# First MoE: three tiles turned ahead of routing, lists loaded between x tiles, and the tail's order of work changed

## The reference

```python
logits = (flat @ router_w).astype(jnp.float32) + router_bias
probs = jax.nn.softmax(logits, axis=-1)
top_w, top_i = jax.lax.top_k(probs, TOPK)               # TOPK = 2 of E = 16
norm_w = top_w / (jnp.sum(top_w, axis=-1, keepdims=True) + 1e-06)
combine = jnp.sum(jax.nn.one_hot(top_i, E) * norm_w[..., None], axis=1)
routed = combine[:, E - 1:E] * flat                      # the last expert is the identity
for e in range(E - 1):
    y = jax.nn.silu(flat @ expert_gate_w[e]) * (flat @ expert_up_w[e]) @ expert_down_w[e]
    routed = routed + combine[:, e:e + 1] * y
gate = conv1d(hidden_states, conv_w)                     # causal, KS = 3 taps
shared = jax.nn.silu(gate) * (hidden_states @ shared_up_w) @ shared_down_w
return shared + routed
```

## Time and profile before

| what | us |
|---|---|
| median of 3 runs (1435.53, 1438.24, 2847.57) | 1438.24 |
| the profiled execution's own time | 1436.97 |
| its span, first to last instruction | 1435.2 |
| TensorE matmul busy in it | 1321.7 (92%) |
| VectorE (DVE) busy | 1008.5 (70%) |
| ScalarE (ACT) busy | 614.5 (43%) |
| GpSimd (POOL) busy | 573.0 (40%) |

### The profile page before, as it was taken

The page is one execution under the profiler, slowest core; times in us unless marked ns, Lnnn a source line. Parts: engine busy times, 40 slices in busy tenths (PEclk is TensorE's granted clock), DMA queues, the critical chain, the costliest instruction groups (busy, mean ns, idle before and its releaser), DMA issues.

```text
span 1435.2 us, 30723 instructions
## 1 busy us (share of the span) xinstructions
PE 1321.7 (92%) x11824; PEld 1087.4 (76%) x11824; DVE 1008.5 (70%) x2390; ACT 614.5 (43%) x1034; POOL 573.0 (40%) x460
## 2 busy tenths in 40 slices
PE   5959998856999999999999899999999999999998
PEld 2449988435888788788788688788788776699974
DVE  5756465377977877876876867877887868655745
ACT  4726555411343333333434344333333656666641
POOL 0536270631323332331441533552553436272635
PEclk9979999978999999999999999999999999999999
DMA  9977695920000000000001000000000038586845
GB/s 324 382 233 247 214 345 205 305 90 1 2 2 2 1 2 1 2 1 2 34 12 61 2 1 2 16 16 1 16 16 1 31 97 302 192 272 214 272 134 154
DMA packets 113628, 150.99 MB, mean 105 GB/s; under 512 B 12240, under 2 KB 96080, under 8 KB 113488
## 3 DMA queue, kind: packets, MB, share of 16 engines
q1 hardware_dynamic: 99088, 113.36, 24.0%
q0 software_dynamic: 12288, 33.57, 7.1%
q10 hardware_dynamic: 2112, 2.10, 0.4%
HBM read 77.56 MB, written 71.43 MB: 104 GB/s over the span
## 4 chain that ended last, share of the span: by engine, by line
PE 61%; DVE 14%; ACT 1%; issue 1%; POOL 0%; DVEq 0%; ACTq 0%
PE l_w_ps L84 9%; PE l_w_ps L86 8%; PE l_w_ps L85 8%; DVE l_probs L2060 5%; PE l_banks L2322 4%; PE l_rm_ps L2354 3%; PE l_banks L84 2%; PE l_banks L85 2%; PE l_banks L86 2%; PE l_rm_ps L2347 2%; PE b_gu_ps L84 2%; PE b_gu_ps L85 1%; PE b_gu_ps L86 1%; DVE l_f_lo L2091 1%; PE b_t_ps L1312 1%; DVE l_full L2022 1%
## 5 line engine op out<-in xcount | busy, mean ns | idle before, releaser
L2060 DVE TENSOR_TENSOR l_probs<-l_banks,l_past 128x512 f32<-128x512 f32 x256 | 160.0, 682 | 35.4 <-PE l_banks L2322 35.3
L1820 ACT ACTIVATE l_act_f<-l_w_ps,l_ffn_b 128x512 f32<-128x512 f32 x120 | 82.6, 689 | 170.5 <-PE l_w_ps L86 165.7
L84 PE MATMUL l_w_ps<-l_w_hi,l_f_hi 128*128 128x256 f32 x496 | 143.7, 290 | 2.6 <-DVE l_f_lo L2091 2.4
L1911 POOL TENSOR_TENSOR l_g_lo<-l_q,l_g_hi 128x1024 fp32r<-128x1024 f32 x16 | 38.2, 2387 | 267.0 <-ACT l_g_hi L1811 267.0
L85 PE MATMUL l_w_ps<-l_w_lo,l_f_hi 128*128 128x256 f32 x496 | 139.6, 282 | 0.0
L86 PE MATMUL l_w_ps<-l_w_hi,l_f_lo 128*128 128x256 f32 x496 | 139.5, 281 | 0.0
L84 PE MATMUL l_w_ps<-l_b_hi,l_w_hi 128*128 128x512 f32 x240 | 102.5, 427 | 0.3 <-ACT l_f_hi L1821 0.3
L1898 POOL TENSOR_TENSOR l_q_wide<-l_q,l_pair_mask 128x1024 f32<-128x1024 f32 x32 | 60.1, 1896 | 103.5 <-DVE l_q L2038 103.5
L812 POOL DMA_INDIRECT rows<-a_xn,a_pos_i x64 | 65.9, 1030 | 86.4 <-DVE a_pos_i L975 67.5
L84 PEld LDWEIGHTS l_w_ps<-l_w_hi,l_f_hi 128*128 128x128 f32 x496 | 93.3, 188 | 8.8 <-issue 8.7
L2091 DVE TENSOR_TENSOR l_f_lo<-l_act_f,l_f_hi 128x512 fp32r<-128x512 f32 x128 | 85.7, 702 | 18.3 <-ACT l_f_hi L1821 18.3
(11 more groups left out here) (428 smaller groups left out, 4000.1 us busy)
## 6 DMA issues: line engine op xcount, KB each, us to landing
rows<-a_zeros SPq DMA_DIRECT2D x14, 1024.0 KB, 12.9
a_xb<-rows SPq DMA_DIRECT2D x46, 256.0 KB, 3.4
rows<-a_yb SPq DMA_DIRECT2D x46, 256.0 KB
b_xb<-rows SPq DMA_DIRECT2D x46, 256.0 KB, 3.3
rows<-b_yb SPq DMA_DIRECT2D x46, 256.0 KB, 3.1
a_w_in<-in_moe_w SPq DMA_DIRECT2D x15, 384.0 KB, 9.1
low_dram<-a_w_lo SPq DMA_DIRECT2D x15, 384.0 KB, 6.7
b_w_lo<-low_dram SPq DMA_DIRECT2D x15, 384.0 KB, 9.0
```

Source lines behind the costliest of these rows:

```text
L84: tensor.matmul(out, w_hi, x_hi, start=start, stop=False)
L1820: nc.scalar.activation(act_f[:, f, :], hidden_ps(b, f), ACT.Gelu, bias=ffn1_b[:, b.layer, f:f + 1]).then_inc(act_done, 1)
L2060: dve.tensor_tensor(probs[c % 2][:, r * w:(r + 1) * w].rearrange("p (h n) -> p h n", n=P), banks[:, r, :].rearrange("p (h n) -> p h n", n= ...
```

## The change

In the head, SP loads x tiles 0 and 2, then lists, bias and router weights, then tiles 4 and 6. TensorE turns tiles 0, 1 and 2, then routes 0 and 1, turns 3, routes 2 and 3.

In the tail, SP stores only tile 0 ahead of the retention's weights and constants, tiles 1 to 3 behind them. DVE does both norms of retention's first tile first, ahead of `shared_product(4)`, and stands the other work in a new order; ACT takes both roots ahead of `shared_gate(4)`, and the high parts of `l_full` and of four pieces ahead of `shared_gate(6)`. TensorE's transposes of retention's tile go to `gu_ps` and stand behind `shared_in(5)`; `shared_in(6)` therefore waits for `first_full`. `combine(c)` may in four places run ahead of `add_shared` of its tile (`added_at`, `early_added`), and `add_shared` then waits for the columns that were to be ahead of it.

The diff:

```diff
--- before.py
+++ after.py
@@ -76,7 +76,6 @@
 GROUPS = (range(3, 8), range(0, 3), range(8, 11), range(11, 15))
 LOW_EARLY = (5, 7)
 NEAR_OLD_AT = 16480
-HOME_SPLITS = ((0, 1), (2, 3), (4, 5), (6,))
 
 
 def split3(tensor, out, w_hi, w_lo, x_hi, x_lo, start, stop):
@@ -379,7 +378,7 @@
             home_hi, home_lo = sem("home_hi"), sem("home_lo")
             first_xn, first_turned, first_full, first_hi = sem("first_xn"), sem("first_turned"), sem("first_full"), sem("first_hi")
             first_lo = sem("first_lo")
-            first_ps = low_ps[:, :, :]
+            first_ps = gu_ps[:, :, :]
 
         taps, pair = TAPS * KD * P, KD * P
         up_at, down_at = taps, taps + pair
@@ -426,16 +425,22 @@
         def part_of(q):
             return int(q >= PAIR0[1])
 
+        def load_tile(engine, t):
+            engine.dma_start(x_sb[:, t * SUB:(t + 1) * SUB, :], tile_view(x_in, t)).then_inc(x_in_done[t], 16)
+
         def sync(sp):
             if begins:
-                for t in range(0, NT, 2):
-                    sp.dma_start(x_sb[:, t * SUB:(t + 1) * SUB, :], tile_view(x_in, t)).then_inc(x_in_done[t], 16)
+                for t in range(0, 4, 2):
+                    load_tile(sp, t)
             else:
                 yield
                 freed(sp, "gated")
             sp.dma_start(lists[:, :], lists_in).then_inc(lists_loaded, 16)
             sp.dma_start(rb[:, :], router_b.partition_broadcast(P)).then_inc(lists_loaded, 16)
             sp.dma_start(rw[:, :, 0:E], router_w.rearrange("(k p) e -> p k e", p=P)).then_inc(lists_loaded, 16)
+            if begins:
+                for t in range(4, NT, 2):
+                    load_tile(sp, t)
 
             def load_piece(n):
                 a = SHARED_COLS + n * EXPERT_COLS
@@ -524,8 +529,11 @@
                 sp.wait_ge(shared_added, t + 1)
                 sp.dma_start(tile_view(out, t), x_sb[:, t * SUB:(t + 1) * SUB, :]).then_inc(stored if t else stored_first, 16)
 
-            for t in TILES_OF[0]:
-                store(t)
+            if begins:
+                store(0)
+            else:
+                for t in TILES_OF[0]:
+                    store(t)
             if begins:
                 sp.wait_ge(acc_done, NPAIRS)
                 sp.wait_ge(low_kept, 16 * PIECES)
@@ -534,6 +542,8 @@
                     if n == 1:
                         for dst, const in consts:
                             sp.dma_start(dst, const).then_inc(consts_in, 16)
+                for t in TILES_OF[0][1:]:
+                    store(t)
             for t in TILES_OF[1][:-1]:
                 store(t)
             for c in range(COLS - SUB, COLS):
@@ -673,7 +683,7 @@
 
             if begins:
                 for t in range(1, NT, 2):
-                    act.dma_start(x_sb[:, t * SUB:(t + 1) * SUB, :], tile_view(x_in, t)).then_inc(x_in_done[t], 16)
+                    load_tile(act, t)
                 root(0)
                 normalise(0)
                 root(1)
@@ -777,19 +787,31 @@
             evacuate(FRONT, True)
             take_y(NPAIRS - 1)
             evacuate(FRONT + 1, True)
-            for t in range(FRONT, NT):
-                shared_gate(t)
-                if begins:
-                    if t < FRONT + 2:
-                        root_ahead(nc, act, ahead, signals, eps, t - FRONT)
-                    for n in HOME_SPLITS[t - FRONT]:
-                        act.wait_ge(home_in[n], 16)
-                        nc.scalar.activation(pieces[n][1], pieces[n][0], ACT.Copy).then_inc(home_hi, 1)
-                if t + 2 < NT:
-                    evacuate(t + 2, True)
-            if begins:
-                act.wait_ge(first_full, 1)
-                nc.scalar.activation(home.a_hi[:, :, :], home.full[:, :, :], ACT.Copy).then_inc(first_hi, 1)
+            if ends:
+                for t in range(FRONT, NT):
+                    shared_gate(t)
+                    if t + 2 < NT:
+                        evacuate(t + 2, True)
+                return
+
+            def high_home(of):
+                for n in of:
+                    act.wait_ge(home_in[n], 16)
+                    nc.scalar.activation(pieces[n][1], pieces[n][0], ACT.Copy).then_inc(home_hi, 1)
+
+            root_ahead(nc, act, ahead, signals, eps, 0)
+            root_ahead(nc, act, ahead, signals, eps, 1)
+            shared_gate(4)
+            high_home(range(0, 2))
+            shared_gate(5)
+            evacuate(6, True)
+            act.wait_ge(first_full, 1)
+            nc.scalar.activation(home.a_hi[:, :, :], home.full[:, :, :], ACT.Copy).then_inc(first_hi, 1)
+            high_home(range(2, 6))
+            shared_gate(6)
+            evacuate(7, True)
+            high_home(range(6, len(pieces)))
+            shared_gate(7)
 
         def gpsimd(pool):
             if begins:
@@ -996,8 +1018,16 @@
                     dve.wait_ge(s_acc_done, t - 1)
                 dve.tensor_tensor(hidden(t), gate_of(t), (gu_ps, t_ps)[t % 2][:, 1, :], ALU.mult).then_inc(sh_done, 1)
 
+            added_at = {4: 20, 5: 23, 6: 27, 7: 28}
+
+            def early_added(c):
+                t = c // SUB
+                return t if c < added_at.get(t, 0) else t + 1
+
             def add_shared(t):
                 dve.wait_ge(s_acc_done, t + 1)
+                if begins and t in added_at and added_at[t] > t * SUB:
+                    dve.wait_ge(x_done, added_at[t])
                 if ends and t >= FRONT:
                     dve.wait_ge(x_done, (t + 1) * SUB)
                 if ends and t == NT - 1:
@@ -1030,7 +1060,7 @@
                                   ALU.subtract).then_inc(h_lo_done, 1)
 
             def combine(c):
-                dve.wait_ge(shared_added, c // SUB + 1 if begins else min(c // SUB + 1, FRONT))
+                dve.wait_ge(shared_added, min(c // SUB + 1, FRONT) if ends else early_added(c))
                 dve.wait_ge(picked_in[c % PICKED], 32 * (c // PICKED + 1))
                 dve.scalar_tensor_tensor(x_sb[:, c, :], picked[:, c % PICKED, 0, :], wk[:, 0, c:c + 1],
                                          x_sb[:, c, :], ALU.mult, ALU.add).then_inc(first_added, 1)
@@ -1182,47 +1212,51 @@
                 finish(range(COLS - 2, COLS))
                 add_shared(NT - 1)
                 return
-            shared_product(4)
             dve.wait_ge(x_done, SUB)
             measure_ahead(dve, ahead, signals, x_sb, 0)
-            finish(range(combined, FRONT * SUB))
-            shared_product(5)
             invert_ahead(dve, ahead, signals, 0)
             dve.wait_ge(signals[3], 1)
             dve.wait_ge(stored_first, 16)
             dve.memset(carrier[:, :], 0.0)
             apply_ahead(dve, ahead, x_sb, lambda s: x_sb[:, s, :]).then_inc(ahead_applied, 1)
-            add_shared(4)
-            finish(range(16, 18))
             dve.wait_ge(ahead_applied, 1)
             measure_ahead(dve, ahead, signals, x_sb, 1)
-            finish(range(18, 20))
-            shared_product(6)
-            add_shared(5)
             invert_ahead(dve, ahead, signals, 1)
             dve.wait_ge(signals[3], 2)
             dve.wait_ge(acc_done, NPAIRS)
             apply_ahead(dve, ahead, x_sb, lambda s: home.xn[:, s, :]).then_inc(first_xn, 1)
-            low_home(range(0, 2))
-            finish(range(20, 22))
-            low_home(range(2, 4))
-            finish(range(22, 24))
-            shared_product(7)
-            low_home(range(4, 6))
+            finish(range(combined, FRONT * SUB))
+            shared_product(4)
+            finish(range(16, 18))
+            low_home(range(0, 1))
+            shared_product(5)
             dve.wait_ge(first_turned, 1)
             dve.wait_ge(consts_in, 16 * len(consts))
             for k in range(KD):
                 last = dve.tensor_scalar(home.full[:, k, :], first_ps[:, k, :], home.norm1[:, 0, 0, k:k + 1],
                                          home.norm1[:, 0, 1, k:k + 1], ALU.mult, ALU.add)
             last.then_inc(first_full, 1)
-            add_shared(6)
-            finish(range(24, 26))
+            finish(range(18, 20))
             dve.wait_ge(first_hi, 1)
             dve.tensor_tensor(home.a_lo[:, :, :], home.full[:, :, :], home.a_hi[:, :, :].bitcast(F32),
                               ALU.subtract).then_inc(first_lo, 1)
+            add_shared(4)
+            low_home(range(1, 3))
+            finish(range(20, 21))
+            shared_product(6)
+            finish(range(21, 23))
+            add_shared(5)
+            finish(range(23, 24))
+            low_home(range(3, 5))
+            finish(range(24, 26))
+            low_home(range(5, 6))
+            finish(range(26, 27))
+            shared_product(7)
+            add_shared(6)
+            finish(range(27, 28))
+            low_home(range(6, len(pieces)))
             add_shared(7)
-            low_home(range(6, len(pieces)))
-            finish(range(26, COLS))
+            finish(range(28, COLS))
 
         def tensor(pe):
 
@@ -1304,6 +1338,8 @@
```

(21 more changed lines are left out.)

## The result

The changed kernel takes 1425.91 us, median of 5 runs (1424.9 to 1428.33); the kernel before took 1435.53 us in 5 runs beside them. One of those five took 2847.57 us; without it their median is 1434.82. The ratio is 0.9934, 95% interval 0.9918 to 0.995: 9.5 us less (7.2 to 11.8). That is under the 2% at which a verdict is drawn, but its interval excludes no change. The profiled execution took 1428.33 us (span 1426.5), 8.64 less than that of before.

The account below looks back on a forecast made before the run. The prediction took DVE to bound the tail's end and TensorE's routes, up to the scatters, the head. From the profiled 1436.97 us, 2.2 (head) and 7.0 (tail) off made 1427.8, stated as 1428.5, range 1425 to 1431.

Parts of the forecast that it names:

- The tail, 7.0 forecast: Tail: with DVE work moved ahead of `shared_product(6)`, the end comes at 305, 7 us less, bounds 3 to 11.
- 8.1 us of DVE's work: Tail: norm, low parts, `l_full` and column 20 leave the stretch behind `shared_product(6)`; 20.0 us stay.
- The wait: Tail: `l_full` waits for all 26 constants, taken in at 272; DVE idles some 6 us in its empty half.
- The 1.5 us added for waits near the end: Tail's end: 1.5 us added, `add_shared(7)` waiting 0 to 1.6 for `shared_down(7)`, DVE's earlier waits about 1.
- The head, 2.2 forecast: Head: 2.2 us less, 1.8 for the hidden route and 0.4 for the earlier start, kept at 0 to 3.
- The step on TensorE: Head: routes 0 and 1 run side by side, the last route ends at 28.0 instead of 30.19.
- the cover: Head: clears in before 43.9 leave 1.7 to 2.2 us for an earlier first scatter; 2.2 was taken.
- rival C: Head gives nothing, constants in the tail come no earlier: 3 us in the tail alone, 1434 to 1435; chance 0.13.
- their price at nothing: Head: x tiles 4 and 6 land later, but this costs nothing, the order ahead of the shared weights being unchanged.
- The picks: Tail: low parts and `l_a_lo` slow eight picks by 1.0 us each, end 306.5; half counted, hidden.

Follow-up runs that it names:

- e9: The changed kernel with the head of before, so only the tail is changed against the kernel before: 1429.29 us against 1434.36, ratio 0.9959.
- e11: The changed kernel with x tiles 6 and 7 loaded behind the eight clears: 1427.2 us, ratio 0.9951 to the kernel before.
- e10: The kernel before with the changed head alone: 1434.68 us against 1434.36, ratio 0.9996.

## Why the prediction was right, and where its steps were off

The time came out within 2.6 us of the forecast, in its own range. Its two terms did less well than their sum: the tail gave 6.0 us for 7.0 and the head 0.4 for 2.2 in the profiled pair, and 3.1 us from a place that no term covers made up for it. The direction and the tail's mechanism were right; that the sum fits this closely is luck.

**The tail, 7.0 forecast.** The mechanism held at each point: 8.1 us of DVE's work left the stretch behind `shared_product(6)`, and 28.1 - 8.1 = 20.0 is what the profiles show there, to a tenth, in the changed kernel, e9 and e11, the three profiles with the changed tail on that kind of chip. The wait came where it was expected, released by a constant, in DVE's empty half. Sizes that were off, in the changed kernel's profile: the last constant is in 6.15 us behind its issue (263.90 to 270.05), where 3.8 was taken (271.16 to 275), but it is also issued earlier, 19.0 in place of 22.8 us behind the loop's last product; `l_full` starts 25.1 us behind that product, against 23.6 by the forecast (272 - 248.4). `shared_in(6)` then began at half the clock and took 8.35 us for its 12 matmuls, more than the 7.75 it was counted by, so `shared_product(6)` came 37.6 us behind the product, not 35.1. The 1.5 us added for waits near the end weren't needed. 35.1 + 20.0 + 1.5 = 56.6 was the forecast for the whole, 57.6 came: 6.0 us gained. In e9 and e11 it was 56.5 and 56.1, so the forecast's 7.0 is within what single executions show.

TensorE stood idle 7.26 us ahead of `shared_in(6)`, and the granted clock was 0.50 (the 1.2 GHz level) for its first 4 us and 1.00 (2.4 GHz) for its last 2. With the same program behind the loop the same 12 matmuls took 7.79 us in e9, after 6.72 us of idleness, and 7.19 in e11, after 6.90. The Trainium skill, "TensorE: Matmul & The Clock Gate", section "What's actually happening", has the low level as what an engine falls back to without activity, and the moment of the change as independent of the kernel. The trace agrees: 8.35, 7.79 and 7.19 us, in no order of the idle times.

**The head, 2.2 forecast.** The step on TensorE held and was undersized (27.15 for 28.0). The step that failed is the cover: "the clears were in before 43.9", so "the first scatter would go at 45.66 - 2.2 = 43.5". It was 45.26, the mechanism of rival C. The landing at 43.96 was read from the order of before, and the change alters that order too: lists, bias and router weights now stand between the x tiles. The prediction put their price at nothing ("the whole order of bytes ahead of the shared weights is as it was"). DMA share and GB/s of the head, before and then after (the last two columns):

```profile
core 0: us, PE busy (x) PEld busy (x) DVE busy (x) ACT busy (x) POOL busy (x), PEclk, DMA share, GB/s
8.00:20.00 12.00, 4.93 (x18) 3.49 (x19) 9.29 (x48) 7.13 (x16) 0.00 (x0) 1.00 1.09 357
20.00:38.00 18.00, 17.31 (x52) 7.13 (x51) 11.10 (x45) 8.85 (x17) 0.00 (x0) 1.00 1.09 386
```

```profile
8.00:20.00 12.00, 5.20 (x22) 4.40 (x23) 9.20 (x47) 7.13 (x16) 0.00 (x0) 1.00 1.04 341
20.00:38.00 18.00, 17.08 (x71) 8.17 (x70) 13.28 (x50) 10.70 (x19) 0.00 (x0) 1.00 1.09 385
```

From 20 to 38 us the 16 DMA engines are full at 385 GB/s in both kernels, so what is lost ahead of 20 is never made up: 357 against 341 GB/s over 12 us are 0.19 MB, or 0.5 us at 385. Over 0 to 44 us it is 330 GB/s before and 323 after, 0.31 MB or 0.8 us at 385. That is the greater part of the 1.3 us by which the first expert piece came later. Most of the loss lies at 8 to 14 us, and it goes with the new order: 306 GB/s in the changed kernel, 299 in e10 and 314 in e11, against 354 before and 352 in e9. Why this order moves fewer bytes was not tested. In e10, with the same head, the clear comes as late (45.48); in e9, with the old head, DVE is the last to come (45.41). The gain on TensorE and the loss in the queue come from the same move, and each takes its share of a cover of 1.7 to 2.2 us. e11 shows the counterpart: with 1 MB less ahead of the clears, the 3.2 us pass as far as the first block load. That this is an earlier end too, as the forecast's sum has it when it takes the head's whole term off the time, is not borne out: the loop gave 2.0 of e11's 2.93 us back, and the medians show none of it.

**The picks.** The forecast counted four extra us for them, hidden. Of the picks' longer rows in the changed tail (1.85 beside the low parts of `l_wp` and `l_wr`, 1.23 beside those of `l_w`, five more of 1.02 to 1.13) the excess over 0.95 sums to 1.8 us. In e9 it is 3.7, with rows of 1.96 and 1.95, and in e11 3.3, so the count of four was near. In the changed kernel it was hidden: behind `shared_product(6)` DVE waited for no pick. The Trainium skill, "SBUF — State Buffer", section "SBUF: two separate sides", would have DVE's two-input operations and a GpSimd operation that reads SBUF exclude each other for whole instructions; in the changed kernel six subtractions of that kind (five low parts and `l_a_lo`, 6.7 us) and 20 column adds of 0.48, which read two SBUF buffers too, ran among the picks, and one pick alone was lengthened by nearly a whole operation, 0.9 us. The trace agrees in kind and not in size.

**What made up the sum.** In the profiled pair: head 0.4, loop 3.1, tail 6.0, and 0.8 given back behind retention's start, 8.7 in all. The 3.1 us in the loop were in no term. Followed by DVE's 46 products, 0.8 of them stand at the first one (12.55 us behind the first block load before, 11.77 after), another 0.8 arise up to the 30th, and 1.5 from the 30th to the 40th. In those ten the DMA engines are full (share 0.97 before and 1.01 after) and the pace is uneven: 37.3 us before, 35.8 in the changed kernel, 36.9 in e9, 35.1 in e10, 36.0 in e11. They don't look like free variation alone: the two profiles with the changed head (the changed kernel and e10) have the loop's last product at 244.93 and 245.07, the two with the old head (before and e9) at 248.40 and 248.30, whatever the tail. The first 0.8 go with the clock: from 90 to 104 us the granted clock is 0.55 before and 0.57 in e9, 0.63 in the changed kernel and in e10, and the first pair's last product stands at 103.91 before and 103.38 in e9, at 102.71 in the changed kernel and 102.86 in e10. But the 12 executions of e10 have the median of before, with its profiled one (1432.39) the fourth from below, so how much of the 3 us belongs to the change in the mean stays open. By the medians the tail alone gives 5.9 us (3.7 to 8.0), the head alone 0.6 (-1.1 to 2.4), the two together 9.5 (7.2 to 11.8): the intervals allow the two parts to add up to all there is, and allow a part of 3 us that only the two together give.

## What to carry to other kernels

Count an engine's work behind the last step that it depends on: moved out of that stretch into an idle one it is worth its own length, to a tenth of a microsecond here, and the price is whatever new wait shifts the step itself, 2.1 us here. When a producer is made earlier, look for the second thing its consumer waits for, and when that comes in the new order: here one queue fed both, its DMA engines were full, and a cover read from the old order didn't hold. An earlier start is not yet an earlier end: of 2.93 us at the loop's start in e11, 0.90 were left at its end. Two halves of a change should be run alone even where their sum comes out as forecast.
